# Values written to the scratch by two queues in turn, scores in sets of three ahead of each strip of values

## The chip, the cores and the metric

One core of one Trainium2 chip. The time is device microseconds of one launch. The kernel before took 717.77 us, the median of three runs (713.58 to 718.51).

## The reference, cut to what matters

The input is two images of 48 x 48 positions with 384 channels. The block is

```
x = x + attention(group_norm(x))      # 12 heads of 32, each query sees a 7 x 7 window
                                      # of positions and 16 registers
x = x + experts(group_norm(x))        # 4 experts, the 2 best of each token, gelu
```

Attention in the reference:

```
qkv = x @ qkv_w.T + qkv_b
k_cat = concat(k, reg_k); v_cat = concat(v, reg_v)
scores = where(mask_cat, q @ k_cat * scale, -1e30)
o = softmax(scores) @ v_cat
out = o @ out_w.T + out_b
```

## The kernel before, in words

Attention runs in six groups (the program's `gi`): two images by three sets of four heads, each set filling 128 channels. An image is cut into six tiles of 8 columns (`s`, "strips" in this text when values and queries are meant) and six bands of 8 rows (`a`). All products are split in a high and a low float16 half, so that each takes three matmuls.

One group passes through these stages:

1. Keys of six bands are computed, split by ScalarE and VectorE, and written by SyncE to a scratch in HBM (`kscr`).
2. Queries of six strips, each written by GpSimd to `qscr`. Between them TensorE projects the output of the group before (`project_out`), which VectorE adds to X (`projected`). SyncE loads keys (KB) and queries (QS) back in the layout of the scores, in the order keys 0, queries 0, keys 1, and so on; its last load of this stage is that of query strip 5.
3. The stage that the change edits. TensorE computes scores of strips 0, 1 and 2 (`scores`, six units of eight matmuls each), of which VectorE takes row maxima (`maximum`, then `split_maxima`); TensorE turns the maxima (`maxima_turned`), ScalarE copies them out (`maxima_out`, MT) and GpSimd puts them into QS (`maxima_in`). In between TensorE computes values of strips 0 to 5 (`values`, 27 matmuls each), ScalarE copies each to one half of the double buffer VT (`values_out`), and GpSimd writes it to `vscr` in three DMAs. A half of VT is written again only once the strip before has landed. SyncE then loads windows of values from `vscr` into VR (`values_in`, six DMAs a strip), which needs the strip itself and the next one.
4. The loop over 36 pairs of strip and band: `key_scores` for the exponentials, `exps` on ScalarE, `weighted` sums on TensorE, with the scores of strips 3 to 5 in between. SyncE loads keys of strips 4 and 5 in it.

Every engine runs its instructions in the order in which the program gives them, and each waits on semaphores: `v_mm` (values computed), `v_sb` (copied to VT), `v_out` (landed in the scratch), `mx` (maxima), `t_ev` (turned maxima copied), `q_out` (queries landed), `st_mm` (exponent scores computed). The scores of strips below 3 use PSUM banks 0, 1, 4, 6, 5, 7 for their six units, values use banks 2 and 3, and the turned maxima bank 7. In groups 2 and 5 the statistics of the next group norm become parameters (`parameters` on VectorE, `deviation` on ScalarE) right before stage 3.

Line numbers of the profile: L1002 scores, L904 all split products, L523 maxima, L770 the copy to VT, L776 the copy to MT, L787 exponentials, L339 GpSimd's write of values, L355 its load of maxima, L230 key writes, L235 and L238 key loads, L244 query loads, L255 value loads, L507 the low half of queries, L451 the last step of the parameters.

Of the kernel before, what the change touches and what calls it, by code (L numbers as in the profile page):

```python
# [10 lines left out]
P = 128  # L11
KC = C // P
# [35 lines left out]
def build(nc, x, wqkv, wo, fc1, fc2, rw, regs, qkb, bv, ob, fb1, fb2, rb, qtab, ktab, gmat, ident16, tri, pick, out):  # L48
    ctx = ExitStack()
    with ctx:  # L50
# [111 lines left out]
        def dve_lows(n, blk):  # L162
# [4 lines left out]
            k_mm k_hi k_lo q_mm q_hi q_lo v_mm v_sb o_mm op_done s_mm mx mxh t_mm t_ev st_mm exd pv sumt rinv norm os_hi os_lo  # L167
# [17 lines left out]
        V_BANK = (2, 3, 2, 3, 2, 3)  # L185
# [5 lines left out]
        S_BANK = lambda s, i: (0, 1, 4, 6, 5, 7)[i] if s < 3 else i % 2  # L191
        PTS = [PT[:, i, :] for i in range(3)] + [QT[:, :, :, :].rearrange("p a b n -> p (a b n)").bitcast(F32)[:, 0:HEADS * 14 * CT_]]

        T_BANK = lambda s: 7 if s < 2 else 1
# [18 lines left out]
        def _(sp):  # L213
# [43 lines left out]
            for gi in range(STAGES):  # L257
# [13 lines left out]
                for s in (0, 1):  # L271
                    values_in(gi, s)
                if gi == 4:
                    sp.dma_start(wr_flat, fc1).then_inc(s_["f_in"], 16)
                if gi == STAGES - 1:
                    for i in range(2):
                        sp.wait_ge(v_out[i], 144 * STAGES)
# [20 lines left out]
        def _(pool):  # L298
# [35 lines left out]
            def values_out(gi, s):  # L334
# [3 lines left out]
                for b in range(KC):  # L338
                    pool.dma_start(vscr[16 * b:16 * b + 16, CT_ * s + 3:CT_ * s + 3 + CT_, :], VT[:, s % 2, b, :]).then_inc(v_out[s % 2], 16)  # L339
# [30 lines left out]
            for gi in range(STAGES):  # L370
# [53 lines left out]
        def _(dve):  # L424
# [136 lines left out]
            for gi in range(STAGES):  # L561
# [18 lines left out]
                for s in range(TILES):  # L580
# [10 lines left out]
                    if gi == 0 and s == 5:  # L591
                        dve.wait_ge(s_["bv_mm"], 1)
                        V.scalar_tensor_tensor(out=cols["obx"], in0=ps[:, 1, 0:KC], scalar=1 / WS, in1=cols["ob"],
                                               op0=ALU.mult, op1=ALU.add).then_inc(s_["obx"], 1)
                    if gi and s:
                        projected(gi - 1, s - 1)
                if gi:
                    projected(gi - 1, TILES - 1)
                if gi in (2, 5):
                    parameters(gi // KC + 1, 0)  # L600
                for s in range(3):
                    for i in range(6):
                        maximum(gi, s, i)
                    split_maxima(gi, s)
# [115 lines left out]
        def _(act):  # L720
# [45 lines left out]
            def values_out(gi, s):  # L766
                act.wait_ge(s_["v_mm"], 6 * gi + s + 1)
                if 144 * gi + 48 * (s // 2) > 0:
                    act.wait_ge(v_out[s % 2], 144 * gi + 48 * (s // 2))
                A(VT[:, s % 2, :, :].rearrange("p b n -> p (b n)"), ps[:, V_BANK[s], 0:SN], ACT.Copy, scale=1 / WS).then_inc(s_["v_sb"], 1)  # L770

            def maxima_out(gi, s):
# [3 lines left out]
                nc.scalar.copy(MT[:, s % 2, :], ps[0:2 * HEADS, T_BANK(s), 0:SN // 2].bitcast(F16)).then_inc(s_["t_ev"], 1)  # L776
# [24 lines left out]
            for gi in range(STAGES):  # L801
# [22 lines left out]
                if gi in (2, 5):  # L824
                    deviation(gi // KC + 1)
                    A(cols["warm"], cols["ob"][:, 0:1], ACT.Exp)
                for s in range(TILES):
                    values_out(gi, s)
                    if s in (1, 3):
                        maxima_out(gi, s // 2)  # L830
# [67 lines left out]
        def _(pe):  # L898
# [28 lines left out]
            def value_bias():  # L927
# [3 lines left out]
                for j in range(KC):  # L931
                    last = split_product(ps[:, 1, j:j + 1], lambda a, k: WO[:, a, k, j * P:(j + 1) * P], lambda b, k: BVH[:, b, k:k + 1])
# [36 lines left out]
            def values(gi, s, b):  # L969
                if b == 0:  # L970
                    if s < 2:
                        pe.wait_ge(s_["q_lo"], 6 * gi + 5 + s)
                    else:
                        pe.wait_ge(s_["v_sb"], 6 * gi + s - 1)
                last = split_product(ps[:, V_BANK[s], P * b:P * (b + 1)], lambda a, k: xh1(a, k, s * SN + b * P, P),
# [294 lines left out]
```

## Time and profile before

| | |
|---|---|
| median of three runs | 717.77 us |
| the profiled execution | 715.22 us, span 713.3 |
| TensorE busy | 593.1 us, 83% |
| VectorE busy | 474.6 us, 67% |
| GpSimd busy | 300.5 us, 42% |
| ScalarE busy | 296.3 us, 42% |
| mean granted clock of TensorE | 0.96 |

A share of busy time is a mean over stages with different limits. Stage 3 of groups 1 to 5 lies at 149.6 to 166.1, 230.8 to 246.7, 314.0 to 333.0, 393.7 to 409.7 and 479.3 to 495.7 us. Group 0 has it from 69.7 to 88.4. The experts follow after the last group, from about 540 us.

### The profile page before, as it was taken

To read this page: it belongs to the slowest core of one execution; us is meant where nothing else is said; L and a number is where in the kernel's file an instruction comes from. 1 tells how busy PE (TensorE), PEld (TensorE's weight loads), DVE (VectorE), ACT (ScalarE), POOL (GpSimd) and SP (SyncE) were. 2 spreads that over 40 slices of the span, in tenths; PEclk is the share of its full clock that TensorE was granted. 3 is DMA by queue.
4 is the path that set the end of the run, shared out by engine and by line. 5 is a ranking of instruction groups with operands and counts; after the bars stand their busy time and mean duration, and the time that the engine had idled before them with its cause. 6 is when DMAs were issued, how large, how long until landed. Compare 5 with 4: busy or idle time off the path is not lost.

```text
span 713.3 us, 22313 instructions
## 1 busy us (share of the span) xinstructions
PE 593.1 (83%) x9225; PEld 413.9 (58%) x9225; DVE 474.6 (67%) x1024; ACT 296.3 (42%) x586; POOL 300.5 (42%) x437
## 2 busy tenths in 40 slices
PE   0686899988997887987898878988777786799997
PEld 0433777667764765566765767557555443455554
DVE  3784566777976699774866768866797476652332
ACT  2343355315632377313552246323584226533231
POOL 4312789235221745318872532216454025621331
PEclk9997999999999999999999989999899898899999
DMA  8959751895359641694429772596520000001102
GB/s 322 277 152 219 203 131 46 215 252 149 92 126 238 187 114 45 164 263 135 123 72 256 209 174 59 123 240 177 152 57 2 1 33 34 34 34 67 66 36 99
DMA packets 130940, 95.93 MB, mean 134 GB/s; under 512 B 67340, under 2 KB 125384, under 8 KB 130072
## 3 DMA queue, kind: packets, MB, share of 16 engines
q1 hardware_dynamic: 121960, 78.72, 42.5%
q0 software_dynamic: 8880, 15.79, 7.4%
q8 instruction: 73, 1.20, 0.7%
q14 instruction: 27, 0.22, 0.1%
HBM read 58.11 MB, written 35.54 MB: 131 GB/s over the span
## 4 chain that ended last, share of the span: by engine, by line
PE 42%; DVE 20%; DMA 15%; ACT 7%; issue 7%; POOL 5%; SPq 3%; ACTq 0%; DVEq 0%; POOLq 0%
PE ps L904 25%; PE ps L1045 6%; DMA qscr<-QT 5%; DMA vscr<-VT 4%; DVE MX L523 4%; PE ps L1026 4%; PE ps L1002 4%; POOL vscr L339 3%; DMA KB<-kscr 2%; DVE GT_ L466 2%; DMA X<-in_x 2%; DVE ST L434 2%; DVE X L517 1%; ACT KB L734 1%; DVE KT L501 1%
## 5 line engine op out<-in xcount | busy, mean ns | idle before, releaser
L523 DVE TENSOR_REDUCE MX<-ps 128x2 f32<-128x456 f32 x216 | 124.4, 626 | 63.3 <-PE ps L1002 62.3
L904 PE MATMUL ps<-XH,WQ 128*128 128x384 f16 x810 | 151.6, 344 | 13.9 <-DVE XH L473 6.4
L904 PEld LDWEIGHTS ps<-XH,WQ 128*128 128x128 f16 x810 | 80.9, 102 | 76.7 <-issue 21.4
L787 ACT ACTIVATE PT<-ps 128x448 f32<-128x448 f32 (+1 forms) x162 | 79.0, 510 | 58.8 <-PE ps L1026 57.7
L1002 PE MATMUL ps<-KB,QS 120*32 120x228 f16 x1728 | 66.1, 276 | 31.9 <-DVE MX L523 9.9
L1026 PE MATMUL ps<-QS,KB 122*128 122x112 f16 (+1 forms) x864 | 65.6, 215 | 17.2 <-ACT VT L770 7.0
L339 POOL DMA_DIRECT2D vscr<-VT x108 | 57.2, 537 | 50.3 <-ACT VT L770 45.9
L409 POOL TENSOR_TENSOR OS<-QS,OS 128x384 f16<-128x384 f32 x36 | 32.3, 912 | 101.6 <-ACT OS L879 101.6
L904 PE MATMUL ps<-OS,WO 128*128 128x384 f16 x324 | 62.4, 343 | 13.3 <-DVE X L517 12.0
L332 POOL DMA_DIRECT2D qscr<-QT x36 | 26.3, 732 | 108.8 <-DVE QT L507 108.8
L1026 PEld LDWEIGHTS ps<-QS,KB 122*128 122x128 f16 x864 | 44.3, 100 | 38.4 <-ACT PT L787 13.0
L904 PE MATMUL ps<-OS,WQ 128*128 128x384 f16 x324 | 61.1, 336 | 6.4 <-POOL KB L317 4.3
L1002 PEld LDWEIGHTS ps<-KB,QS 120*32 120x32 f16 x1728 | 38.0, 99 | 46.4 <-DVE MX L523 14.7
L355 POOL DMA_DIRECT2D QS<-MT x72 | 38.2, 537 | 61.4 <-ACT MT L776 61.2
L1045 PE MATMUL ps<-PT,VR 128*32 128x112 f32 (+1 forms) x1296 | 61.7, 264 | 1.1 <-issue 0.8
L904 PE MATMUL ps<-WQ,XH 128*128 128x128 f16 x972 | 59.6, 223 | 0.8 <-issue 0.8
L1045 PE MATMUL ps<-PT,ONE 128*32 128x112 f32 (+1 forms) x1296 | 59.5, 258 | 0.0
L904 PEld LDWEIGHTS ps<-WQ,XH 128*128 128x128 f16 x972 | 56.2, 100 | 4.7 <-issue 4.7
L675 DVE TENSOR_TENSOR QS<-ps,QS 128x384 f32<-128x384 f32 x36 | 19.6, 554 | 53.6 <-POOL OS L409 27.7
L904 PEld LDWEIGHTS ps<-OS,WO 128*128 128x128 f16 x324 | 32.2, 102 | 39.4 <-issue 18.9
L517 DVE SCALAR_TENSOR_TENSOR X<-ps,X 128x384 f32<-128x384 f32 x108 | 53.0, 549 | 2.0 <-PE ps L904 1.2
L770 ACT ACTIVATE VT<-ps 128x384 f32<-128x384 f32 x36 | 17.7, 490 | 87.7 <-PE ps L904 55.4
(159 smaller groups left out, 978.7 us busy)
## 6 DMA issues: line engine op xcount, KB each, us to landing
KB<-kscr SPq DMA_DIRECT2D x108, 192.0 KB, 7.0
kscr<-KT SPq DMA_DIRECT2D x72, 192.0 KB, 2.5
VR<-vscr SPq DMA_DIRECT2D x216, 56.0 KB
QS<-qscr SPq DMA_DIRECT2D x108, 96.0 KB, 5.6
X<-in_x SPq DMA_DIRECT2D x6, 1152.0 KB, 18.9
qscr<-QT POOLq DMA_DIRECT2D x36, 192.0 KB, 5.1
vscr<-VT POOLq DMA_DIRECT2D x108, 64.0 KB, 2.3
out<-X SPq DMA_DIRECT2D x12, 576.0 KB, 3.3
```

The source lines that it names most:

```text
L332: pool.dma_start(qscr.rearrange("a p n -> p a n")[:, :, s * SN:(s + 1) * SN], QT[:, s % 2, :, :]).then_inc(q_out[s % 2], 16)
L339: pool.dma_start(vscr[16 * b:16 * b + 16, CT_ * s + 3:CT_ * s + 3 + CT_, :], VT[:, s % 2, b, :]).then_inc(v_out[s % 2], 16)
L355: pool.dma_start(QS[SROWS + part:SROWS + part + 1, :, s * SN:(s + 1) * SN], MT[part * HEADS:(part + 1) * HEADS, s % 2, :]).then_inc(m_in[s ...
L409: nc.gpsimd.tensor_tensor(HW[:, m % 2, 1, k, :], HF[:, unit % 2, :], HW[:, m % 2, 0, k, :], ALU.subtract).then_inc(s_["hl"], 1)
L517: V.scalar_tensor_tensor(out=xj, in0=ps[:, OP_BANK(gi, s, j), 0:SN], scalar=1 / WS, in1=xj, op0=ALU.mult, op1=ALU.add).then_inc(s_["op_don ...
L523: V.tensor_reduce(out=MX[:, s % 2, t, 2 * pair:2 * pair + 2], in_=ps[:, S_BANK(s, i), 0:2 * RUN].rearrange("p (h n) -> p h n", h=2), op=AL ...
L675: V.tensor_tensor(HF[:, unit % 2, :], ps[:, 2 + k, 0:SN], GE[:, unit % 2, :], ALU.mult).then_inc(s_["hf"], 1)
L787: A(PTS[n % 4][:, 0:w], ps[:, ST_BANK(n), 0:w], ACT.Exp, scale=SCORE).then_inc(s_["exd"], 1)
L904: last = mm(bank, lhsT(a, k), rhs(b, k), start=(k == 0 and n == 0), stop=(finish and k == steps - 1 and n == 2))
L1002: last = mm(ps[32 * j:32 * j + 32, S_BANK(s, i), hh * RUN:(hh + 1) * RUN], QS[0:SROWS, h, q0:q0 + 32], KB[0:SROWS, h, slot(s), CHUNK * a:C ...
L1026: last = mm(ps[:, ST_BANK(n), h * w:(h + 1) * w], KB[0:TROWS, h, slot(s), LEAD + CHUNK * a:LEAD + CHUNK * (a + 1)], QS[0:TROWS, h, s * SN ...
L1045: last = mm(ps[DH * h:DH * (h + 1), bank, CT_ * q0:CT_ * q1], lhsT, PTS[n % 4][:, h * w:(h + 1) * w], start=(a == 0), stop=(a == STRIPS - ...
```

## The change

- In groups 1 to 5, SyncE writes the odd value strips and GpSimd the even ones. A new semaphore `v_sp` counts SyncE's. On SyncE the write of strip 1 stands ahead of the value loads of strip 0, that of strip 3 ahead of the value loads of strip 1, and that of strip 5 behind them.
- TensorE computes three score units, then a strip of values, six times over. In group 0 it computes three strips of values first.
- Values of strip 5 go to bank 1 in groups 1 to 5; turned maxima always go to bank 0.
- The parameters of groups 2 and 5 are computed after query strip 3, instead of after strip 5.
- The bias product of group 0 (`value_bias`, bank 7 instead of 1) comes after the first three value strips.

SyncE's queue in group 1, from the last query loads (QS) on. Before, where vscr is the scratch and VR the windows:

```order
L244 DMA QS<-qscr 32x4x384 x9
L255 DMA VR<-vscr 112x1x128 x12
L235 DMA KB<-in_ktab 8x4x868
L238 DMA KB<-kscr 32x4x768 x3
L255 DMA VR<-vscr 112x1x128 x6
```

Of the change, the same place:

```order
L246 DMA QS<-qscr 32x4x384 x9
L253 DMA vscr<-VT 16x8x128 x3
L266 DMA VR<-vscr 112x1x128 x6
L253 DMA vscr<-VT 16x8x128 x3
L266 DMA VR<-vscr 112x1x128 x6
L253 DMA vscr<-VT 16x8x128 x3
L237 DMA KB<-in_ktab 8x4x868
L240 DMA KB<-kscr 32x4x768 x3
```

Three sets of three writes now stand between query loads and the key load of strip 4, the second of them behind the first six value loads.

TensorE in group 1. Before (QS and KB: scores; XH: values; ID: turned maxima; the last row is the first exponent scores):

```order
L1002 MATMUL ps<-KB,QS 32x228 x48
L904 MATMUL ps<-WQ,XH 128x128 x54
L1012 MATMUL ps<-ID,MXH 8x128 x3
L1002 MATMUL ps<-KB,QS 32x228 x48
L904 MATMUL ps<-WQ,XH 128x128 x54
L1012 MATMUL ps<-ID,MXH 8x128 x3
L1002 MATMUL ps<-KB,QS 32x228 x48
L904 MATMUL ps<-WQ,XH 128x128 x54
L1026 MATMUL ps<-QS,KB 128x88 x4
```

Of the change:

```order
L1038 MATMUL ps<-KB,QS 32x228 x24
L932 MATMUL ps<-WQ,XH 128x128 x27
L1038 MATMUL ps<-KB,QS 32x228 x24
L932 MATMUL ps<-WQ,XH 128x128 x27
L1038 MATMUL ps<-KB,QS 32x228 x24
L932 MATMUL ps<-WQ,XH 128x128 x27
L1038 MATMUL ps<-KB,QS 32x228 x24
L1050 MATMUL ps<-ID,MXH 8x128 x3
L932 MATMUL ps<-WQ,XH 128x128 x27
L1038 MATMUL ps<-KB,QS 32x228 x24
L932 MATMUL ps<-WQ,XH 128x128 x27
L1038 MATMUL ps<-KB,QS 32x228 x24
```

The rows keep their number of matmuls in sum; a strip of values (27) now follows each half of a strip of scores (24).

The diff, cut to its core:

```diff
-        V_BANK = (2, 3, 2, 3, 2, 3)
+        V_BANK = lambda gi, s: 1 if gi and s == TILES - 1 else 2 + s % 2
...
+            def values_out(gi, s):        # SyncE
+                sp.wait_ge(s_["v_sb"], 6 * gi + s + 1)
+                sp.wait_ge(s_["pv"], 36 * gi)
+                for b in range(KC):
+                    sp.dma_start(value_rows(s, b), VT[:, s % 2, b, :]).then_inc(s_["v_sp"], 16)
...
             def values_in(gi, s):
                 for t in {s, min(s + 1, TILES - 1)}:
-                    sp.wait_ge(v_out[t % 2], 144 * gi + 48 * (t // 2 + 1))
+                    if gi and t % 2:
+                        sp.wait_ge(s_["v_sp"], 144 * (gi - 1) + 48 * (t // 2 + 1))
+                    else:
+                        sp.wait_ge(v_out[t % 2], 144 * gi + 48 * (t // 2 + 1))
...
                 for s in (0, 1):
+                    if gi:
+                        values_out(gi, 2 * s + 1)
                     values_in(gi, s)
+                if gi:
+                    values_out(gi, 5)
...
             # GpSimd
+                if gi:
+                    register_values(gi)
                 for s in range(TILES):
-                    values_out(gi, s)
-                    if s == 1:
-                        register_values(gi)
-                    if s in (1, 3):
-                        maxima_in(gi, s // 2)
+                    if gi == 0 or s % 2 == 0:
+                        values_out(gi, s)
+                    if gi and s in (3, 5):
+                        maxima_in(gi, s // 4)
+                if gi == 0:
+                    register_values(gi)
+                    for s in (0, 1):
+                        maxima_in(gi, s)
...
             def values_out(gi, s):        # ScalarE
                 act.wait_ge(s_["v_mm"], 6 * gi + s + 1)
-                if 144 * gi + 48 * (s // 2) > 0:
-                    act.wait_ge(v_out[s % 2], 144 * gi + 48 * (s // 2))
+                if gi and s % 2:
+                    act.wait_ge(v_out[1], 144)
+                    if 144 * (gi - 1) + 48 * (s // 2) > 0:
+                        act.wait_ge(s_["v_sp"], 144 * (gi - 1) + 48 * (s // 2))
+                else:
+                    if 144 * gi + 48 * (s // 2) > 0:
+                        act.wait_ge(v_out[s % 2], 144 * gi + 48 * (s // 2))
...
             def scores(gi, s, i):         # TensorE
-                if i == 5 and s in (1, 2) or i == 1 and s >= 3:
+                if i == 0 and s == 2:
+                    pe.wait_ge(s_["t_ev"], 6 * gi + 1)
+                if i == 0 and s == 3:
+                    pe.wait_ge(s_["v_sb"], 6 * gi + 6)
+                if i == 1 and s >= 3:
                     pe.wait_ge(s_["t_ev"], 6 * gi + s)
...
             def key_scores(gi, n):
                 if n < 2:
-                    pe.wait_ge(s_["v_sb"], 6 * gi + n + 5)
+                    pe.wait_ge(s_["v_sb"], 6 * gi + (5 if gi else 6))
...
-                for s in range(TILES):
-                    if s % 2 == 0:
-                        if s:
-                            maxima_turned(gi, s // 2 - 1)
-                        for i in range(6):
-                            scores(gi, s // 2, i)
+                def three_scores(k):
+                    for i in range(3):
+                        scores(gi, k // 2, 3 * (k % 2) + i)
+                    if k in (3, 5):
+                        maxima_turned(gi, k // 2 - 1)
+
+                def all_values(s):
                     for b in range(KC):
                         values(gi, s, b)
+
+                if gi == 0:
+                    for s in range(3):
+                        all_values(s)
+                    value_bias()
+                for k in range(6):
+                    three_scores(k)
+                    if gi:
+                        all_values(k)
+                    elif k < 3:
+                        all_values(3 + k)
```

## Rows read from the trace of the kernel before

**Rows 1.** The page, busy time of the engines, share of the span, instructions

```profile
PE 593.1 (83%) x9225; PEld 413.9 (58%) x9225; DVE 474.6 (67%) x1024; ACT 296.3 (42%) x586; POOL 300.5 (42%) x437
```

**Rows 2.** Busy time by stretch: stretch, length, engines, clock, DMA share, GB/s; group 4, five groups' sum

```profile
393.70:409.70 16.00, 14.10 (x317) 12.79 (x316) 11.57 (x26) 3.54 (x9) 9.63 (x19) 1.00 0.76 207
...
sum 83.80, PE 71.74 PEld 65.56 DVE 56.89 ACT 19.56 POOL 52.13; mean PE 14.35 PEld 13.11 DVE 11.38 ACT 3.91 POOL 10.43
```

**Rows 3.** Timeline of ScalarE in group 4: start, length, instruction, idle time before it

```profile
398.22 0.49 ACT L770 ACTIVATE VT<-ps 128x384 f32<-128x384 f32 x1 [1.02 <-PE ps L904]
...
408.78 1.02 ACT L770 ACTIVATE VT<-ps 128x384 f32<-128x384 f32 x2 [3.75 <-PE ps L904]
409.69 1.11 ACT L787 ACTIVATE PT<-ps 128x352 f32<-128x352 f32 x2
```

**Rows 4.** Timeline of SyncE: the last query loads of groups 1 to 5, group 1's value loads

```profile
155.41 2.28 SPq L244 DMA_DIRECT2D QS<-qscr  x3
160.60 8.43 SPq L255 DMA_DIRECT2D VR<-vscr  x12
...
234.65 2.47 SPq L244 DMA_DIRECT2D QS<-qscr  x3
...
319.56 2.06 SPq L244 DMA_DIRECT2D QS<-qscr  x3
...
399.94 1.25 SPq L244 DMA_DIRECT2D QS<-qscr  x3
...
483.30 2.16 SPq L244 DMA_DIRECT2D QS<-qscr  x3
```

**Rows 5.** Timeline of ScalarE: the first exponentials of groups 1, 2, 3 and 5

```profile
166.09 1.11 ACT L787 ACTIVATE PT<-ps 128x352 f32<-128x352 f32 x2
...
246.72 0.46 ACT L787 ACTIVATE PT<-ps 128x352 f32<-128x352 f32 x1
...
332.99 1.11 ACT L787 ACTIVATE PT<-ps 128x352 f32<-128x352 f32 x2
...
495.73 0.46 ACT L787 ACTIVATE PT<-ps 128x352 f32<-128x352 f32 x1
```

**Rows 6.** By line: key writes (L230) and landing, min/median/max; landing of value writes (L339)

```profile
L230 SPq DMA_DIRECT2D kscr<-KT x72: 512/631/1966, 34.1 to 462.3; - x72
...
DMA to landing us min/median/max: 2.4/2.5/6.9
...
DMA to landing us min/median/max: 1.9/2.3/5.2
```

**Rows 7.** The chain of waits in group 5: start, length, what

```profile
500.41 1.89 DMA vscr<-VT
...
506.84 4.02 DMA KB<-kscr
```

**Rows 8.** By line L1002, what scores waited for: us in all, times

```profile
  DVE SM L451: 3.9, 2
```

**Rows 9.** Busy time by stretch, in group 0 and group 2; columns as in rows 2

```profile
89.80:93.20 3.40, 3.40 (x68) 2.83 (x72) 0.86 (x2) 1.64 (x4) 3.37 (x5) 0.51 0.21 59
93.20:96.40 3.20, 3.20 (x116) 2.72 (x112) 2.10 (x5) 1.45 (x4) 3.20 (x4) 1.00 0.88 201
246.70:250.10 3.40, 3.22 (x51) 2.53 (x55) 1.45 (x3) 3.30 (x8) 2.62 (x5) 0.51 0.43 130
```

**Rows 10.** Timeline of group 0: GpSimd's first value writes, ScalarE's third and fifth copy, exponentials

```profile
74.85 3.17 POOL L339 DMA_DIRECT2D vscr<-VT  x6 [4.67 <-ACT VT L770]
...
79.22 0.49 ACT L770 ACTIVATE VT<-ps 128x384 f32<-128x384 f32 x1 [2.81 <-DMA vscr<-VT]
...
83.58 0.49 ACT L770 ACTIVATE VT<-ps 128x384 f32<-128x384 f32 x1 [2.62 <-DMA vscr<-VT]
...
88.44 0.90 ACT L787 ACTIVATE PT<-ps 128x352 f32<-128x352 f32 x2
```

**Rows 11.** The chain of waits in group 0

```profile
68.53 0.62 DVE QT L507
```

More of the change, by code:

```diff
@@ L275, in _ @@
                 if gi == STAGES - 1:
-                    for i in range(2):
-                        sp.wait_ge(v_out[i], 144 * STAGES)
+                    sp.wait_ge(v_out[0], 144 * STAGES)
+                    sp.wait_ge(s_["v_sp"], 144 * (STAGES - 1))
                     for src, dst in ((fc2, f2raw), (rw, rwraw)):
@@ L338, in values_out @@
                 for b in range(KC):
-                    pool.dma_start(vscr[16 * b:16 * b + 16, CT_ * s + 3:CT_ * s + 3 + CT_, :], VT[:, s % 2, b, :]).then_inc(v_out[s % 2], 16)
+                    pool.dma_start(value_rows(s, b), VT[:, s % 2, b, :]).then_inc(v_out[s % 2], 16)
             def register_values(gi):
@@ L590, in _ @@
                         V.tensor_tensor(BVH[:, 1, :], cols["bv"], BVH[:, 0, :], ALU.subtract).then_inc(s_["bvlo"], 1)
[L591 to L594, printed above, removed]
                     if gi and s:
                         projected(gi - 1, s - 1)
+                    if gi in (2, 5) and s == 3:
+                        parameters(gi // KC + 1, 0)
                 if gi:
                     projected(gi - 1, TILES - 1)
-                if gi in (2, 5):
-                    parameters(gi // KC + 1, 0)
                 for s in range(3):
@@ L603, in _ @@
                         maximum(gi, s, i)
+                        if gi == 0 and s == 0 and i == 2:
+                            dve.wait_ge(s_["bv_mm"], 1)
+                            V.scalar_tensor_tensor(out=cols["obx"], in0=ps[:, 7, 0:KC], scalar=1 / WS, in1=cols["ob"],
+                                                   op0=ALU.mult, op1=ALU.add).then_inc(s_["obx"], 1)
                     split_maxima(gi, s)
@@ L823, in _ @@
                         A(BVH[:, 0, :], cols["bv"], ACT.Copy).then_inc(s_["bvhi"], 1)
-                if gi in (2, 5):
-                    deviation(gi // KC + 1)
-                    A(cols["warm"], cols["ob"][:, 0:1], ACT.Exp)
+                    if gi in (2, 5) and s == 3:
+                        deviation(gi // KC + 1)
+                        A(cols["warm"], cols["ob"][:, 0:1], ACT.Exp)
                 for s in range(TILES):
                     values_out(gi, s)
-                    if s in (1, 3):
-                        maxima_out(gi, s // 2)
+                    if gi and s in (2, 4):
+                        maxima_out(gi, s // 2 - 1)
+                if gi == 0:
+                    for s in (0, 1):
+                        maxima_out(gi, s)
                 n = {2: 1, 5: 2}.get(gi)
@@ L972, in values @@
                         pe.wait_ge(s_["q_lo"], 6 * gi + 5 + s)
+                    elif gi and s == TILES - 1:
+                        pe.wait_ge(s_["mx"], 36 * gi + 14)
                     else:
                         pe.wait_ge(s_["v_sb"], 6 * gi + s - 1)
-                last = split_product(ps[:, V_BANK[s], P * b:P * (b + 1)], lambda a, k: xh1(a, k, s * SN + b * P, P),
+                last = split_product(ps[:, V_BANK(gi, s), P * b:P * (b + 1)], lambda a, k: xh1(a, k, s * SN + b * P, P),
                                      lambda q, k: WQ[:, gi % KC, q, k, 2 * P:3 * P])
```

25 lines of the change are left out of this document (14 added, 11 removed).

## The prediction

> **What bounds the kernel now.** I read the page first, then busy time by stretch, then what ScalarE, SyncE and GpSimd do in those stretches, and last the chain. The reader should see on the page that no engine is full: TensorE is busy 83% of 713.3 us and the others less [rows 1]. So waits decide, and I looked for the stretch that the edits touch. In each of the six head groups it reaches from the first score matmul to the first exponential. In groups 1 to 5 that is 83.8 us in all, 16.0 of them in group 4, in which TensorE works 14.1 [rows 2]. That leaves 12 us to win, over five groups. What fills it is seen on ScalarE [rows 3]: value strip 1 is copied at 398.22, the last two at 408.78, and the first exponential starts at 409.69. A strip must land in the scratch before its half of VT is written again.
>
> The second thing to see is SyncE's queue [rows 4]. In group 4 it issues query loads until 399.94 + 1.25 = 401.19; twelve value loads follow, which took 8.43 us in group 1. So SyncE is not idle when value strip 1 is ready (398.22 + 0.49 = 398.7): it is then still 2.5 us from the end of its query loads, the last of which waits for a query strip that lands late. I call that end E. It is 157.69, 237.12, 321.62, 401.19 and 485.46 in groups 1 to 5, and the first exponentials start at 166.09, 246.72, 332.99, 409.69 and 495.73 [rows 5], which is 8.40, 9.60, 11.37, 8.50 and 10.27 after E: 48.1 us in sum.
>
> **The change, part by part.** *Odd strips on SyncE (groups 1 to 5).* The order on SyncE becomes: query loads, write of strip 1, six value loads, write of strip 3, six value loads, write of strip 5. ScalarE's copy of strip 5 goes into the half of VT that strip 3 leaves, so it waits until strip 3 has landed. Queued behind that copy on ScalarE are all exponentials; the first score unit of strip 3 of the loop waits for the same copy, and TensorE with it. The new path, from E:
> - three issues of strip 1. The trace has no such issue on SyncE; the nearest is the key write, same direction and same queue, median 0.63 us, landing 2.5 us later [rows 6]. The last starts at E + 1.3. Here the queue still holds query loads, so I take 3.0 for the landing: E + 4.3.
> - six value loads that wait for it: twelve take 8.43 us [rows 4], so 4.2: E + 8.5.
> - strip 3's three issues, the last starting at E + 9.8, landing 2.5 later: E + 12.3.
> - ScalarE's copy; the exponential starts 0.4 after the copy's start (the two copies from 408.78 take 1.02 with the wait between them, so the second starts at 409.3 [rows 3]): E + 12.7.
>
> Five groups at 12.7 are 63.5, against 48.1: **+15.4 us**. Bounds: issues at 0.42 (three query loads take 1.25 [rows 4]) with the shortest landing of a value write, 1.9 [rows 6], give 0.8 + 1.9 + 4.2 + 0.8 + 1.9 + 0.4 = 10.0 per group, +1.9 in all. Issues at 0.70 (a value load's share of the 8.43) and landings of 4.5 and 3.5 (key writes go up to 6.9) give 1.4 + 4.5 + 4.2 + 1.4 + 3.5 + 0.4 = 15.4, +28.9. I stay nearest the key write.
>
> In group 5 the last part is hidden: the next long wait of TensorE there ends with a key load that SyncE may issue only after the weights of the second layer, and those wait for the last value strip, landed at 502.3 [rows 7]. Strip 5's write on SyncE comes at E + 8.5 + 1.9 + 4.2 = E + 14.6, and lands about 3.8 later, at 503.9. So this group loses about 1.3 instead of 2.4: **-1.1**.
>
> *Scores in sets of three before each value strip.* The same 144 score matmuls and 162 value matmuls in another order: nothing on TensorE itself. It takes away the stall of TensorE on the bank of the turned maxima and needs six steps of about 2.3 us (14.1 over six), so values end about 14 us after the first score. That is ahead of the new path (in group 4, E is 7.5 after the first score at 393.7, so the exponential comes at 20.2). Cost and gain nothing; if SyncE's path were gone, this is what would show.
>
> *Group statistics two query strips earlier (groups 2 and 5).* Scores waited 3.9 us for them in two places [rows 8]. They would start that much earlier, but E hangs on the query round trip and not on the first score, so the gain is swallowed: 0. With the cover gone it would be -3.9.
>
> *TensorE's clock.* With values done at +14 and the exponential at +20, TensorE stands some 5 us in every group. Behind TensorE's stops at the end of this stage in group 0 the granted clock was 0.51 for 3.4 us (the 1.2 GHz level), 68 matmuls, where 116 ran in the next 3.2 us at 1.00 (2.4 GHz) [rows 9]: 68 would have taken 1.9, so 1.5 us lost. Group 2 already has such a stretch behind its first exponential [rows 9], and group 5 is covered by the key load. Three groups at 1.5: **+4.5**. Bounds 0 (each hidden by a later wait) and 7.5.
>
> *Group 0* opens with three value strips, which run while the queries come back. The second of them waits for the low half of query strip 5, which ends at 68.53 + 0.62 = 69.15 [rows 11], so about then TensorE turns to the rest of the stage, as it does now. The value writes start some 4 us earlier (now 74.85 [rows 10]) but the queue of GpSimd now has all 18 of them, then two register copies, and only then the maxima, for which the first exponent scores wait. By pairs of strips, 4.4 us apart (copies at 79.22 and 83.58 [rows 10]): second pair copied at 75 to 79, third at 79.4 to 83.6, its last strip 1.5 later, written in 1.9, then 2.1 for registers and the first maxima, 2.4 to land and 0.4 to the exponential: 88 to 92, against 88.44. I take **+1.5**, bounds -1 and +4.
>
> Sum: 15.4 - 1.1 + 4.5 + 1.5 = +20.3. The profiled execution took 715.22 us, span 713.3, so it gives 735.5; the median shown is 717.77, 2.5 above. I forecast **735**. A measurement of this kernel can tell about 1% from no change, that is 710.6 to 724.9.
>
> **Rivals.** (a) *Faster: the issuing engine was the limit.* If SyncE got to strip 1 at 399 instead of at E, for instance because query strip 5 lands sooner, GpSimd's writes and SyncE's run side by side, and the stage shrinks to TensorE's own time: 83.8 - 71.7 = 12.1 [rows 2], plus 3.9 for the earlier statistics, 699 us. For it: the wait for value writes to land stands on the chain, even at the last strip of group 5 [rows 7]. It begins to win where SyncE gets to strip 1 more than 3.1 us before E (12.7 on the new path against 48.1 / 5 = 9.6). Against it: the order on SyncE and three waits for landing in a row. The Trainium skill, Perfetto Trace Analysis, section DMA Optimizations, says that if descriptor generation is the bottleneck, balancing DMAs across engines may help; by that rule the change gains. In group 4 GpSimd is busy 9.63 of 16.0 us [rows 2], so this case's trace bears it out only in part. Chance 0.10.
>
> (b) *No change: the short end.* Issues cost 0.42, landings 1.9 to 2.2, and no loss of clock: +3 to +6, group 0 at 0: about 720. For it: query loads are issued in 0.42 on this queue. Against it: key writes take 0.63 there and value loads 0.70. Chance 0.16. The Trainium skill, DMA: Bandwidth & Descriptors, section Issuing engines are not separate DMA queues, says that issuing on several engines saves only the sequencer's time, since all share the same 16 DMA engines; by it alone, the result lies near this case.
>
> (c) The forecast, with its own range 724 to 748: chance 0.74, of which 0.72 is beyond 1%.
>
> **Range and chances.** The range leaves out (a) and the ends of (b) and (c): 718 to 746. Faster 0.10, within 1% 0.18, slower 0.72.
>
> **What would show it.** Right: in groups 1 to 5 ScalarE's sixth copy of VT waits for "DMA vscr<-VT" issued on SyncE, and starts 10 to 15 us after the last query load; the key loads for strips 4 and 5 start later by about the same; TensorE idles 4 to 6 us before the first exponential and its clock is halved behind it; scores start 1.8 us earlier against the projections in groups 2 and 5. Wrong: if SyncE's writes of strip 1 start before the last query load, if the sixth copy waits for TensorE, or if the delay at the first exponential is taken back by a later wait, as in group 5 in part; then each group's length, and not its start, tells.

## The result: 3.4% slower, and the profile after

The changed kernel takes 743.23 us, the median of four runs (737.49 to 751.23), against 717.44 us for the kernel before on the same chip: ratio 1.034, 95% interval 1.026 to 1.043. Measured once more on another chip it took 739.7 us (737.79 to 741.98), ratio 1.035 (1.028 to 1.042). The first profile is of the 751.23 us execution, an outlier of its four, so all rows of "after" below are of the second measurement, profiled at 737.79 us with a span of 735.3: 22.0 longer than the 713.3 of before.

The page of after, engines busy, answers to [rows 1]. Busy times are nearly the same (TensorE +3.3 us, GpSimd less, for 45 writes have left it), and the span is longer: the time went into waits.

```profile
PE 596.4 (81%) x9225; PEld 418.6 (57%) x9225; DVE 477.2 (65%) x1024; ACT 296.6 (40%) x586; POOL 278.0 (38%) x392
```

Busy time by stretch, first score to first exponential, group 4 and the sum over groups 1 to 5 (columns as in [rows 2]). The stretch grew from 16.0 to 19.5 us, the five from 83.8 to 99.0; TensorE's part hardly moved (71.7 to 74.1).

```profile
407.60:427.06 19.46, 14.67 (x321) 12.92 (x320) 11.84 (x26) 3.55 (x9) 6.90 (x13) 0.95 0.66 169
...
sum 99.00, PE 74.05 PEld 64.74 DVE 59.37 ACT 17.71 POOL 35.34; mean PE 14.81 PEld 12.95 DVE 11.87 ACT 3.54 POOL 7.07
```

The timeline of ScalarE in that stretch (start, length, instruction, idle time before it and who ended it) answers to [rows 3]. The sixth copy into VT, at 426.66, now waits 4.63 us for a value write to land; the exponential starts behind it.

```profile
412.32 0.49 ACT L795 ACTIVATE VT<-ps 128x384 f32<-128x384 f32 x1 [1.82 <-PE ps L932]
...
421.20 0.49 ACT L795 ACTIVATE VT<-ps 128x384 f32<-128x384 f32 x1 [1.83 <-DMA vscr<-VT]
...
426.66 0.49 ACT L795 ACTIVATE VT<-ps 128x384 f32<-128x384 f32 x1 [4.63 <-DMA vscr<-VT]
427.05 0.90 ACT L812 ACTIVATE PT<-ps 128x352 f32<-128x352 f32 x2
```

SyncE's timeline beside it, from the last query loads to the key load of strip 4. Value strip 1 was copied at 412.81, and its write is issued at 415.37, when the query loads (9.15 us in one piece) are through; the write of strip 3 stands behind six value loads.

```profile
406.12 9.15 SPq L246 DMA_DIRECT2D QS<-qscr  x9
415.37 1.85 SPq L253 DMA_DIRECT2D vscr<-VT  x3
418.82 4.25 SPq L266 DMA_DIRECT2D VR<-vscr  x6
423.17 1.85 SPq L253 DMA_DIRECT2D vscr<-VT  x3
425.13 4.23 SPq L266 DMA_DIRECT2D VR<-vscr  x6
429.46 2.77 SPq L253 DMA_DIRECT2D vscr<-VT  x3
...
433.29 1.26 SPq L240 DMA_DIRECT2D KB<-kscr  x3
```

By line, the new issues: length min/median/max in ns, and landing in us.

```profile
L253 SPq DMA_DIRECT2D vscr<-VT x45: 565/598/1583, 159.1 to 520.5; - x45
...
DMA to landing us min/median/max: 2.0/2.5/3.9
```

Who TensorE waited for, in us, times, longest; of before and then of after. New is the wait of scores (L1038) for the VT copy, 19.6 us in five times, once in each of groups 1 to 5.

```profile
PE ps L1002 <- DMA KB<-kscr: 7.9, 3, 4.2
PE ps L1026 <- ACT VT L770: 7.0, 7, 2.4
```

```profile
PE ps L1038 <- ACT VT L795: 19.6, 5, 5.1
...
PE ps L1038 <- DMA KB<-kscr: 10.1, 7, 3.1
```

The 22.0 us by stages, from the two traces: first exponential of group 0 +2.0 (88.4 to 90.4); first score to first exponential, groups 1 to 5, +15.2; first to last exponential, all groups, +7.0; last exponential to the next group's first score -3.2; experts after the last exponential +0.9.

### The profile page after: what moved, and what is told of

Its sections match the earlier page's. It is cut to its first block, busy times and chain, and to the rows that moved or that the text cites. A ratio compares the mean times of both kernels' runs of the same rounds, so it can differ in the third digit from the quotient of the medians.

```text
span 748.8 us, 22314 instructions
## 1 busy us (share of the span) xinstructions
PE 604.6 (81%) x9225; PEld 422.4 (56%) x9225; DVE 477.0 (64%) x1024; ACT 296.8 (40%) x586; POOL 277.2 (37%) x392
## 4 chain that ended last, share of the span: by engine, by line
PE 39%; DMA 20%; DVE 17%; SPq 8%; issue 7%; ACT 5%; POOL 2%; ACTq 0%; DVEq 0%; POOLq 0%
PE ps L932 24%; DMA qscr<-QT 6%; DMA vscr<-VT 6%; PE ps L1083 5%; DMA KB<-kscr 5%; SPq L266 4%; PE ps L1064 3%; PE ps L1038 3%; DVE MX L543 3%; DVE GT_ L486 3%; DMA X<-in_x 2%; SPq L253 2%; DVE ST L454 2%; PE ps L940 1%; POOL vscr L354 1%
## 5 line engine op out<-in xcount | busy, mean ns | idle before, releaser
L543 DVE TENSOR_REDUCE MX<-ps 128x2 f32<-128x456 f32 x216 | 126.1, 628 | 89.7 <-PE ps L1038 88.4
L932 PE MATMUL ps<-XH,WQ 128*128 128x384 f16 x810 | 147.0, 337 | 17.6 <-DVE XH L493 9.3
L932 PEld LDWEIGHTS ps<-XH,WQ 128*128 128x128 f16 x810 | 79.8, 100 | 77.2 <-issue 16.8
L1038 PE MATMUL ps<-KB,QS 120*32 120x228 f16 x1728 | 69.1, 281 | 48.8 <-ACT VT L795 18.2
L1038 PEld LDWEIGHTS ps<-KB,QS 120*32 120x32 f16 x1728 | 35.3, 99 | 66.1 <-issue 31.0
L932 PE MATMUL ps<-OS,WQ 128*128 128x384 f16 x324 | 64.5, 348 | 6.5 <-POOL KB L332 4.5
L932 PE MATMUL ps<-WQ,XH 128*128 128x128 f16 x972 | 63.8, 226 | 7.1 <-DVE QT L527 4.3
L1064 PEld LDWEIGHTS ps<-QS,KB 122*128 122x128 f16 x864 | 46.0, 103 | 35.2 <-issue 15.0
L1083 PE MATMUL ps<-PT,VR 128*32 128x112 f32 (+1 forms) x1296 | 63.8, 273 | 0.9 <-DMA VR<-vscr 0.8
L1083 PE MATMUL ps<-PT,ONE 128*32 128x112 f32 (+1 forms) x1296 | 61.8, 267 | 0.0
L795 ACT ACTIVATE VT<-ps 128x384 f32<-128x384 f32 x36 | 17.6, 490 | 109.5 <-DMA vscr<-VT 65.4
L354 POOL DMA_DIRECT2D vscr<-VT x63 | 33.3, 534 | 65.0 <-ACT VT L795 65.0
L932 PEld LDWEIGHTS ps<-OS,WO 128*128 128x128 f16 x324 | 31.9, 101 | 43.1 <-issue 22.6
L695 DVE TENSOR_TENSOR QS<-ps,QS 128x384 f32<-128x384 f32 x36 | 19.6, 555 | 55.3 <-POOL OS L429 28.7
## 6 DMA issues: line engine op xcount, KB each, us to landing
X<-in_x SPq DMA_DIRECT2D x6, 1152.0 KB, 18.5
```

What stands on the lines that cost most here:

```text
L354: pool.dma_start(value_rows(s, b), VT[:, s % 2, b, :]).then_inc(v_out[s % 2], 16)
L543: V.tensor_reduce(out=MX[:, s % 2, t, 2 * pair:2 * pair + 2], in_=ps[:, S_BANK(s, i), 0:2 * RUN].rearrange("p (h n) -> p h n", h=2), op=AL ...
L932: last = mm(bank, lhsT(a, k), rhs(b, k), start=(k == 0 and n == 0), stop=(finish and k == steps - 1 and n == 2))
L1038: last = mm(ps[32 * j:32 * j + 32, S_BANK(s, i), hh * RUN:(hh + 1) * RUN], QS[0:SROWS, h, q0:q0 + 32], KB[0:SROWS, h, slot(s), CHUNK * a:C ...
L1064: last = mm(ps[:, ST_BANK(n), h * w:(h + 1) * w], KB[0:TROWS, h, slot(s), LEAD + CHUNK * a:LEAD + CHUNK * (a + 1)], QS[0:TROWS, h, s * SN ...
L1083: last = mm(ps[DH * h:DH * (h + 1), bank, CT_ * q0:CT_ * q1], lhsT, PTS[n % 4][:, h * w:(h + 1) * w], start=(a == 0), stop=(a == STRIPS - ...
```

## The experiments

Ratios are to the kernel before on the same chip, with 95% intervals: 713.53 us on the chip of the first four, 714.41 on the next four's, 713.37 on the last three's. Two theories are set against each other in most of them. P: the first exponential waits for the sixth VT copy, and that for strip 3's write behind the value loads (the prediction's path). Q: what limits is SyncE's in-order queue as a whole, in which the key loads of strips 4 and 5 stand last.

**1. Only the writes moved, on the kernel before.**

```diff
+                    if gi:
+                        values_out(gi, 2 * s + 1)
                     values_in(gi, s)
+                if gi:
+                    values_out(gi, 5)
...
-                    values_out(gi, s)
+                    if gi == 0 or s % 2 == 0:
+                        values_out(gi, s)
```

> The kernel before, with one part of the change alone: in groups 1 to 5 SyncE writes the odd value strips, in the same order on SyncE as in the change. TensorE's order is the old one. Theory P (path: query loads, write 1, six loads, write 3, then ScalarE's copy of strip 5): the first exponential stands 12 to 13 us after SyncE's last query load, as in the change, and the time is 735 to 745. Rival O (the new order on TensorE costs the time, the path only fills what that leaves): the time stays at 715 to 722.

734.98 us (734.37 to 736.4), ratio 1.030 (1.028 to 1.033). The moved writes alone cost 21.5 us, nearly the whole loss. In the profile it stands at the first exponentials: 15.5 us later behind E (the end of SyncE's last query load) in sum of groups 1 to 5, the loops only 1.1 longer; the experts' part adds 5.4, of which the last section speaks.

**2. All of the change but the moved writes.** GpSimd writes every strip; SyncE's loads are those of before.

```diff
-                    if gi:
-                        values_out(gi, 2 * s + 1)
                     values_in(gi, s)
-                if gi:
-                    values_out(gi, 5)
...
-                    if gi == 0 or s % 2 == 0:
-                        values_out(gi, s)
+                    values_out(gi, s)
```

> The change without its SyncE part: GpSimd writes all value strips again in all groups, in the new order of everything else (sets of three, group 0 opened with values, parameters early, the maxima loads behind strips 3 and 5). Theory P: the whole loss lies in SyncE's part, so the time is that of the kernel before or a little less, 712 to 720; group 0 may cost its 1 to 3 us. Rival O: 735 or more.

725.17 us (720.66 to 727.17), ratio 1.016 (1.012 to 1.020). That is above theory P's 712 to 720 and below rival O's 735: the rest of the change costs 1.6%, where the forecast gave it 1.5 us. The two parts don't add up: 3.0% and 1.6% by themselves, 3.5% together.

**3. Strip 3's write ahead of the value loads.**

```diff
+                if gi:
+                    values_out(gi, 1)
+                    values_out(gi, 3)
                 for s in (0, 1):
-                    if gi:
-                        values_out(gi, 2 * s + 1)
                     values_in(gi, s)
```

> The change, with the write of strip 3 ahead of the first six value loads on SyncE; the same instructions otherwise. Theory P: strip 1 landed at E + 3.9, copied strip 3 at E + 4.4, its last write starts at E + 5.8 and lands at E + 8.3, the first exponential comes at E + 8.7 in place of 12.5; five times 3.8 is 19 us less, about 724. Rival Q (the loss is the length of SyncE's queue, which holds up the key loads of strips 4 and 5): the queue is as long as before, so 740 or more.

744.06 us (742.62 to 745.74), ratio 1.044 (1.040 to 1.047): no gain at all, where theory P had about 724. The wait that I had named is nearly gone (2.4 us), and another has its place. TensorE's waits:

```profile
PE ps L1039 <- DMA KB<-kscr: 26.1, 5, 8.2
...
PE ps L1039 <- ACT VT L796: 2.4, 5, 0.7
```

and SyncE's timeline in group 4. The six writes wait for strip 3's copy and hold the queue for 7.5 us; loads of values, and behind them those of keys, come later (key loads of strip 4 by 6.2 us in sum).

```profile
414.62 7.48 SPq L253 DMA_DIRECT2D vscr<-VT  x6
422.22 8.89 SPq L266 DMA_DIRECT2D VR<-vscr  x12
431.21 2.80 SPq L253 DMA_DIRECT2D vscr<-VT  x3
```

**4. A buffer of its own for strip 5, so that its copy waits for no landing.** Strip 5 is copied to RINV, which is free until the first normalization of the group. The order on SyncE is the change's.

```diff
-                    sp.dma_start(value_rows(s, b), VT[:, s % 2, b, :]).then_inc(s_["v_sp"], 16)
+                    sp.dma_start(value_rows(s, b), RINV[:, b * P:(b + 1) * P] if s == 5 else VT[:, 1, b, :]).then_inc(s_["v_s5" if s == 5 else "v_sp"], 16)
...
+                    if s == 5:
+                        act.wait_ge(s_["norm"], 6 * gi)
```

> The change, with strip 5 copied to a third buffer (the memory of RINV), so that its copy waits for no landing. SyncE's order is unchanged. Theory P alone: the first exponential comes at about 14 us after the first score, 6 us earlier than in the change, five times that is 30, so 713 to 718. P together with Q: the first exponential does come that early, but the key load of strip 4 still starts 17 us after E, so TensorE waits for it inside the loop, and the time is 733 to 740.

737.25 us (735.72 to 738.97), ratio 1.034 (1.031 to 1.037), the change's own. First exponentials came 9.8 us earlier behind the last query load (sum of five groups 54.9 against 64.7) and the loops took 10.3 us more (192.6 against 182.3). I had expected 30 us earlier against the first score; it was 8.4 (90.6 against 99.0). The edit brings a wait of its own, of VectorE's first normalizations for strip 5's landing, 2.8 us in all. TensorE's wait for keys is far longer:

```profile
PE ps L1043 <- DMA KB<-kscr: 24.2, 7, 8.0
```

**5. The change again**, for a profile beside the others.

> The change itself once more, for a second profile and times on the chip of the next three. Theory: as measured, 737 to 745; the first exponential 12 to 13 us behind SyncE's last query load, and 17 to 18 us from that load to the first key load of strip 4 (12 to 15 in the kernel before).

739.7 us, ratio 1.035 (1.028 to 1.042); its rows are those above.

**6. Early group statistics alone, on the kernel before.**

```diff
+                    if gi in (2, 5) and s == 3:
+                        parameters(gi // KC + 1, 0)
                 if gi:
                     projected(gi - 1, TILES - 1)
-                if gi in (2, 5):
-                    parameters(gi // KC + 1, 0)
```

> The kernel before, with the group statistics of groups 2 and 5 taken two query strips earlier, alone. Theory (the stage hangs on the query strips' way back, not on the first score): scores start 1.5 to 2 us earlier against the last projection, the first exponential less than 1 us earlier, the time within 2 us of the kernel before. Rival: the 3.9 us that the scores waited come back in full, 709 to 711.

713.18 us (706.73 to 716.4, ten runs), ratio 0.997 (0.992 to 1.002): no difference. Scores did come 4.2 us sooner between the groups (154.9 against 159.1 in sum), and the stretches up to the first exponential grew by 5.2. Swallowed, as forecast: E itself came only 1.6 us sooner in sum.

**7. The change, but group 0 in sets of three like the others.**

```diff
                 if gi == 0:
-                    for s in range(3):
-                        all_values(s)
                     value_bias()
...
                     three_scores(k)
-                    if gi:
-                        all_values(k)
-                    elif k < 3:
-                        all_values(3 + k)
+                    all_values(k)
...
             # GpSimd
-                    if gi and s in (3, 5):
+                    if gi == 0 and s == 1:
+                        register_values(gi)
+                    if s in (3, 5):
                         maxima_in(gi, s // 4)
-                if gi == 0:
-                    register_values(gi)
-                    for s in (0, 1):
-                        maxima_in(gi, s)
```

> The change, with group 0 in the order of the other groups (sets of three scores, then a strip of values; maxima loaded behind value strips 3 and 5), not opened with values; GpSimd still writes all six strips in group 0. Theory: opening with values costs the first exponential of group 0 about 2 us (91.2 in the change against 88.4), so this one is 1 to 4 us faster than the change, 738 to 742. Rival: the opening gains, and without it the first exponential comes later than 91.2.

732.81 us (732.07 to 734.1), ratio 1.026 (1.019 to 1.032), beside 739.7 for the change on the same chip; I had expected a smaller gain, 738 to 742. Timeline of ScalarE in group 0, first of after, then of this kernel: the exponential comes 4.3 us sooner, though values started later. In after it stands behind TensorE, which stands behind maxima that GpSimd sends only when all 18 writes and two register copies are issued. The edit takes away both the opening with values and this place of the maxima loads; no run separates them.

```profile
81.94 1.06 ACT L795 ACTIVATE VT<-ps 128x384 f32<-128x384 f32 x2 [3.58 <-DMA vscr<-VT]
...
85.94 0.47 ACT L801 COPY MT<-ps 8x384 f16<-8x384 f16 x1 [2.13 <-PE ps L1050]
...
90.39 0.92 ACT L812 ACTIVATE PT<-ps 128x352 f32<-128x352 f32 x2 [2.68 <-PE ps L1064]
```

```profile
81.97 0.47 ACT L799 COPY MT<-ps 8x384 f16<-8x384 f16 x1 [0.37 <-PE ps L1045]
84.27 0.49 ACT L793 ACTIVATE VT<-ps 128x384 f32<-128x384 f32 x1 [1.83 <-DMA vscr<-VT]
...
86.07 0.90 ACT L810 ACTIVATE PT<-ps 128x352 f32<-128x352 f32 x2
```

GpSimd's and TensorE's timelines of after in the same place, the last value writes, the register copies, the maxima, and TensorE's wait for them:

```profile
82.72 3.14 POOL L354 DMA_DIRECT2D vscr<-VT  x6 [2.22 <-ACT VT L795]
85.85 1.06 POOL L364 DMA_DIRECT2D VR<-VRG  x2
86.88 2.04 POOL L370 DMA_DIRECT2D QS<-MT  x4
```

```profile
89.91 0.83 PE L1064 MATMUL ps<-QS,KB 122*128 122x88 f16 x8 [4.00 <-DMA QS<-MT]
```

**8. ScalarE as the second issuer, with early statistics, on the kernel before.**

```diff
             # GpSimd
-                    values_out(gi, s)
+                    if gi == 0 or s not in (1, 3):
+                        values_out(gi, s)
...
             # ScalarE
                     values_out(gi, s)
...
+                    if gi and s in (1, 3):
+                        act.wait_ge(s_["v_sb"], 6 * gi + s + 1)
+                        act.wait_ge(s_["pv"], 36 * gi)
+                        for b in range(KC):
+                            act.dma_start(vscr[16 * b:16 * b + 16, CT_ * s + 3:CT_ * s + 3 + CT_, :], VT[:, 1, b, :]).then_inc(s_["v_sp"], 16)
```

> The kernel before with early group statistics, and in groups 1 to 5 value strips 1 and 3 written by DMAs that ScalarE issues behind its copies, strip 5 and the even ones by GpSimd. SyncE's queue keeps its old length, and GpSimd's loses six issues of 0.53 us. Theory Q (what costs is the length of SyncE's queue, not that a second queue writes): no slower than the kernel before, 705 to 718. Rival (any second queue costs, since the writes land no sooner): 725 or more.

712.32 us (710.67 to 716.14, ten runs), ratio 0.997 (0.994 to 1.000). Six writes a group from ScalarE, whose queue has copies and exponentials behind them but none of these loads, cost nothing; nine from SyncE cost 3%. A gain is not shown either.

**9. Three writes a group on SyncE, where nothing of P is touched.**

```diff
                 for s in (0, 1):
                     values_in(gi, s)
+                if gi:
+                    values_out(gi, 5)
```

> The kernel before, with one edit: in groups 1 to 5 the values of strip 5 are written by SyncE (three DMAs), after both sets of value loads; GpSimd writes strips 0 to 4. This gives SyncE a third of the change's writes at a place where neither the first exponential nor any value load of strips 0 and 1 stands behind them. Theory P (the change is slow because the first exponential waits for the sixth VT copy, and that for strip 3's writes behind the query loads): here strip 3 is GpSimd's again, first exponential after the last query load as before (48.2 us over five groups), time as before, ratio 0.997 to 1.003. Theory Q (what limits is the length of SyncE's queue: each DMA issued there costs 0.42 to 0.70 us, and the first key loads of strips 4 and 5 and the loads of strip 2's values stand behind it): three issues of 0.6 us and the wait for strip 5's copy push the first key load of strip 4 by 2 to 3 us a group, of which the loop takes what its reserve does not hold; the first exponential unmoved, the loops longer by 4 to 10 us in sum, ratio 1.006 to 1.014.

719.0 us (716.54 to 725.3, ten runs), ratio 1.010 (1.007 to 1.014), as theory Q asks. The key loads of strip 4 came 10.7 us later in sum, and the loops took 4.4 more; of the 11.9 us that TensorE waited for keys, 11.2 stand in groups 4 and 5. The first exponentials came 4.0 us later behind E too, where I expected none. Experiments 6 and 8, in the same order and with no write on SyncE, show 2.6 and 1.8 of it (table); the rest is open. SyncE and TensorE in group 4:

```profile
406.35 8.74 SPq L266 DMA_DIRECT2D VR<-vscr  x12
415.19 3.07 SPq L251 DMA_DIRECT2D vscr<-VT  x3
...
419.32 1.26 SPq L238 DMA_DIRECT2D KB<-kscr  x3
```

```profile
427.32 0.95 PE L1024 MATMUL ps<-KB,QS 120*32 120x228 f16 x16 [5.67 <-DMA KB<-kscr]
```

**10. Sets of three in all six groups, no writes on SyncE**: the edits of 2 and 7 together, with the early statistics.

> The change without its SyncE part (GpSimd writes all values) and with group 0 in sets of three like the others, so not opened with values: what is left of the change is the sets of three ahead of each strip of values, the banks, and the early group statistics. Against the kernel with GpSimd writing everything and group 0 opened with values, 725.17 us and 1.0161 of the kernel before, this differs in group 0 alone. Theory G (opening group 0 with values costs about 7 us, as the pair 739.7 and 732.8 showed with SyncE writing): ratio 1.003 to 1.009. Rival S (the sets of three themselves cost, in groups 1 to 5, and group 0 was not the cause): ratio 1.013 or more. The forecast had both at +1.5 and 0 us.

717.55 us (715.1 to 721.07, ten runs), ratio 1.007 (1.004 to 1.010). Beside experiment 2 (1.016) this confirms group 0's price (theory G) with another pair: 0.9%, some 6 us, though four runs stand against ten there, and 4.6 us between the two profiles lie in the experts' part, which no edit touches. And it sizes what is left of the change, sets of three with their banks and the later maxima loads: some 0.7% slower than before. The stretches up to the first exponential grew by 9.1 us in sum (83.8 to 92.9), of which the loops gave back 3.6. One wait is new with this order, that of the exponent scores for the maxima: 12.4 us here and 16.6 in experiment 2, against 0.5 in before. GpSimd sends them behind strips 3 and 5, where before sent them behind 1 and 3. What the order of scores costs without that, no run shows.

```profile
PE ps L1046 <- DMA QS<-MT: 12.4, 8, 2.9
```

**11. The same with ScalarE's six writes of experiment 8**, the candidate to beat both.

> The kernel of the run beside it (sets of three in all groups, early group statistics), with strips 1 and 3 of groups 1 to 5 written by DMAs that ScalarE issues right behind its copy of the strip; GpSimd writes strips 0, 2, 4 and 5, SyncE writes nothing. It is the candidate for a version that beats both. If dividing the writes is of use where the second issuer has no loads behind them, the copies of strips 3 and 5 wait less for GpSimd's queue, the loops shorten by up to the 5 us that ScalarE's writes gave on the order of the kernel before (168.9 against 173.9), ratio 0.993 to 1.001. If ScalarE's six issues a group delay its own copies and the maxima behind them, ratio 1.003 or more, the first exponentials later by 6 x 0.6 us at most a group.

719.8 us (713.46 to 724.28, twelve runs), ratio 1.007 (1.004 to 1.010): not better than 10, so the candidate failed. Its first exponentials weren't later (51.6 us behind E in sum, against 53.0), so the rival's reason isn't seen either; its loops took 180.7 us against 171.7. Of these 9.0 us 5.5 stand in group 3, where TensorE waited 4.7 us in one piece for maxima (3.1 in experiment 10), after GpSimd had stood 2.4 us between two writes of one strip for nothing that the profile shows, and had 6.8 us of half clock behind it. The rest is open. The best that these runs have is the order of before, with or without experiment 8's edits.

**All of it in one table.** Sums over groups 1 to 5, in us, worked out from each trace. E is the end of SyncE's last query load. "Score waits" are TensorE's in the score matmuls, for the VT copy and for key loads, from the view of waits over all six groups; a dash is a wait that the view doesn't list.

| kernel | ratio | writes on SyncE per group | E to key load of strip 4 | E to first exponential | first to last exponential | E to last exponential | score waits: VT, keys |
|---|---|---|---|---|---|---|---|
| before | 1 | 0 | 73.3 | 48.2 | 175.3 | 223.5 | -, 7.9 |
| 6 | 0.997 | 0 | 75.6 | 50.8 | 173.9 | 224.8 | -, 8.1 |
| 8 | 0.997 | 0 | 73.0 | 50.0 | 168.9 | 218.9 | -, 3.8 |
| 10 | 1.007 | 0 | 72.6 | 53.0 | 171.7 | 224.7 | 0.4, - |
| 11 | 1.007 | 0 | 72.5 | 51.6 | 180.7 | 232.2 | 4.3, 2.0 |
| 2 | 1.016 | 0 | 72.6 | 51.5 | 175.0 | 226.5 | 0.4, 1.9 |
| 9 | 1.010 | 3 | 84.0 | 52.2 | 179.7 | 231.9 | -, 11.9 |
| 1 | 1.030 | 9 | 95.3 | 63.7 | 176.4 | 240.1 | -, 7.0 |
| 7 | 1.026 | 9 | 95.8 | 65.1 | 176.6 | 241.7 | 16.6, 6.7 |
| after | 1.035 | 9 | 95.6 | 64.7 | 182.3 | 247.0 | 19.6, 10.1 |
| 4 | 1.034 | 9 | 98.0 | 54.9 | 192.6 | 247.5 | -, 24.2 |
| 3 | 1.044 | 9 | 101.8 | 50.1 | 199.3 | 249.4 | 2.4, 26.1 |

In the order of before the VT copy is awaited by the exponent scores instead: 7.0 us in before, 18.5 in 1, 10.8 in 9. Read the last three rows: the first exponential moves by 15 us, the last doesn't (247.0 to 249.4). What tells is how far the key load stands behind the first exponential, the difference of two columns: 31 to 32 us in 9, 1, 7 and after, with 7 to 12 us of waits for keys; 43.1 in 4, with 24.2; 51.7 in 3, with 26.1. In 1 and 7 the late key loads cost nothing more than in before, since the loop itself starts late; they bind when the loop starts early. The run that would test this alone, key loads ahead of the writes on SyncE, wasn't made.

45 issues of 0.598 us are 26.9 us, and the key loads of strip 4 moved by 22.3 in sum; 15 are 9.0, and they moved by 10.7.

How fine may the table be read? Rows 7 and after run the same instructions in groups 1 to 5 and differ by 5.3 us at the last exponential; the first profile of the change has 247.8 there. The clock doesn't explain the 5.3: from E to the last exponential half clock lasted 37.3 us in 7 and 34.4 in after. TensorE's waits for keys (6.7 and 10.1) and, in groups 1 to 5, for maxima (none and 2.2) differ by about that, and why they do is open. Row 11 too is late, with no late key load.

## Why the prediction was right, and where it wasn't

The time was forecast at 735 in a range of 718 to 746, with 0.72 on slower; it came out at 743 and 740. On the profiled executions the sum was +20.3 us, measured +22.6 (715.22 to 737.79). Some luck is in that total: parts that were put at nothing or at 1.5 us cost 1.6% by themselves (experiment 2), but came covered by the path.

- **The new path from E** was right in its steps, within 0.9 us each. Forecast +15.4; from E to the first exponential the two profiles of the change have 62.7 and 64.7 for the forecast 63.5, against 48.2 of before. In group 4, against E = 415.27, the strip 1 issues end at +1.95 (forecast 1.9), value loads start at +3.6 (4.3), strip 3's issues start at +7.9 (8.5), the exponential at +11.8 (12.7). In group 4 strip 1 lay ready 2.5 us before E and waited for the queue, as the prediction said against rival (a). An issue takes 0.60 us where I had 0.63, a landing 2.5. Experiment 1, with the writes alone, has 63.7: 15.5 of the 16.6 us that it loses up to the last exponentials.
- **What the path is worth** was wrong, and the total hid it. I took the rest of SyncE's queue for uncritical. The key loads of strips 4 and 5 stand in it too, behind nine more issues. Experiments 3 and 4 take the path away, 14.6 and 9.8 us of it, and get nothing back: a second bound of the same size stood right behind. Experiment 9 shows it by itself, in small (loops 4.4 us longer, of which 4.0 are waits for keys). So both are true: the path sets the time of the change as it is, and mending it would not help. For the mended version of experiment 3 the path alone gave about 724, and it takes 744.
- **Group 5 covered, -1.1**: not seen. From E to the last exponential the group took 55.3 us, against 52.4: 2.9 lost, where I had 1.3 (and my own times, 503.9 against 502.3, give 1.6). In the chain of waits of group 5 in after, which answers to [rows 7], strip 5's landing ends at 523.15 and the key load's at 531.23: 19.6 and 27.6 us after E (503.6), where before had 16.8 and 25.4 after its E. The order of these waits was right and the size short: I had the landing at +18.4, and it moved by 2.7, the key load behind it by 2.2.

```profile
504.95 3.58 DMA vscr<-VT
...
512.92 2.30 DMA vscr<-VT
...
520.47 2.68 DMA vscr<-VT
...
526.71 4.52 DMA KB<-kscr
```

- **TensorE's clock, +4.5**: of the right kind, the size not borne out. Half clock (1.2 GHz) stands behind the stop at the first exponential in all five groups, 3.4 us in groups 1, 2, 3 and 5 and 6.8 in group 4, where it began within the stop. Busy time by stretch in group 1, columns as in [rows 9]: TensorE had stood 4.0 us, then 58 matmuls ran at 0.50, then 111 at 1.00.

```profile
167.00:172.40 5.40, 1.36 (x30) 1.13 (x27) 0.52 (x3) 1.66 (x5) 2.70 (x5) 1.00 0.45 128
172.40:175.80 3.40, 3.40 (x58) 2.80 (x56) 3.07 (x6) 1.64 (x5) 1.03 (x2) 0.50 0.33 91
175.80:179.20 3.40, 3.40 (x111) 2.83 (x112) 2.89 (x6) 1.89 (x5) 0.00 (x0) 1.00 0.55 136
```

  Up to the last exponential half clock lasted 52.0 us, against 34.1. What this cost no run separates. The loops of groups 1 to 5 grew by 7.0 us, of which the waits for keys (2.2 more over all groups) and for maxima (1.7 more) are a part. Experiments 1 and 7 had more half clock in these loops too, 26.7 and 28.2 us against 17.1 in before, and their loops grew by 1.1 and 1.3 us alone: there the slower matmuls were nearly all hidden, as the bound of 0 had it. So this term may well have been too large, and the loops' waits have filled its place.
- **Group 0, +1.5**: measured +2.0 at the first exponential, in bounds. But it was reckoned against the order of before, and sets of three bring the first exponential sooner there, at 86.07 and 86.75 us in experiments 7 and 10 against 88.44. Beside them opening with values, with the maxima behind all writes, costs 6 to 7 us of the total, 3.4 to 4.3 of which stand at the first exponential. Where the rest lies isn't settled.
- **Sets of three, 0**: covered in the change, as forecast. With the cover gone they cost (experiment 10, +0.7%). I had said that values would then end about 14 us after the first score; the sixth copy starts at 17.6 in the mean of five groups, against 16.4 in before.
- **Early statistics, 0**: right (experiment 6), and for the reason given, since E moved by 1.6 us only.

The chance of 0.10 for rival (a) was fair in that experiment 8 shows the writes can be divided without loss; that there is a gain in it, no run shows. By the Trainium skill, DMA: Bandwidth & Descriptors, section Issuing engines are not separate DMA queues, issuing on several engines saves only the time that the sequencer takes to issue. That time, 0.6 us an issue, is what moved here, 45 times, and it moved in front of loads; these runs agree with the page in that no version gained.

## What to carry to other kernels

An issue that moves to another queue delays what stands behind it there: count how many issues are put ahead of each load that something waits for, and price each at its length, not only the one path that looks longest. Before mending the wait that a trace shows, ask what in the same queue would come due next; here the mended kernel is no faster, since the key loads came due next. If writes must move, try a queue with none of the loads behind them (six a group on ScalarE cost nothing in the order of before), or leave them.

## What the runs showed beside that

The experts' part after the last exponential is the same program in all kernels, and came in two lengths: 175.5 to 177.3 us in seven profiles and 180.7 to 181.9 in six. TensorE's half clock in it was 20.5 to 27.1 us in the seven and 33.9 to 35.1 in the six. Busy time over that part, of before and of experiment 2: nearly the same number of matmuls, 5.3 us more busy, granted clock 0.94 and 0.90.

```profile
537.86:713.30 175.44, 147.88 (x1084) 87.09 (x1072) 86.47 (x188) 61.80 (x112) 51.89 (x54) 0.94 0.11 41
```

```profile
543.41:725.30 181.89, 153.19 (x1096) 90.39 (x1088) 86.31 (x188) 61.80 (x112) 51.87 (x54) 0.90 0.11 40
```

So 5 us of a single profile may be the place where half clock falls and not the edit; the stages before it, and medians of ten runs, are what a difference of 1% should rest on. Experiments 1, 2, 3, 8 and 9 and the first profile of the change are on the long side. For 9 it shows: the profiled execution took 725.12 us, the median of its ten 719.0.
